# Edits to a recommendation tower: the Gram products by single samples in two runs per block, transposed by VectorE straight from PSUM; unit moves all on ScalarE

## What is computed

```python
e = stack([tbl_f[ids[:, f]] for f in range(26)], axis=1)          # 2048 x 26 x 128
all_emb = concatenate([r_bottom_output[:, None, :], e], axis=1)   # 2048 x 27 x 128
gram = einsum('bfd,bgd->bfg', all_emb, all_emb)
z = gram[:, TRIU_I, TRIU_J]                                       # 351 pairs, k=1
h = concatenate([z, r_bottom_output], axis=1)                     # 479
h = maximum(h @ W_top1 + b_top1, 0)                               # 512
h = maximum(h @ W_top2 + b_top2, 0)                               # 256
y = h @ W_top3                                                    # 1
```

## Time and profile before

| | us |
|---|---|
| three runs | 396.2, 398.02, 399.08 (median 398.02) |
| profiled execution | 398.24, its span 396.4 |
| TensorE clock granted, mean over the span | 0.99 |

### The profile page before, as it was taken

One profiled execution on the slowest core, in us unless ns is written; L12 is line 12 of the kernel. 1 busy time (PEld: TensorE's weight loads), 2 busy tenths in 40 slices (PEclk: granted clock), 3 DMA queues, 4 the chain that ended last, 5 costly groups with the idle time before them and its releaser, 6 DMA issues.

```text
span 396.4 us, 10314 instructions
## 1 busy us (share of the span) xinstructions
PE 364.6 (92%) x4064; PEld 333.9 (84%) x4064; DVE 284.1 (72%) x817; ACT 226.4 (57%) x438; POOL 263.0 (66%) x281
## 2 busy tenths in 40 slices
PE   0878979999998999899979999899998999999997
PEld 0767869988988989799978989799897999998886
DVE  5999998987678776784567676767767687644342
ACT  3446857764654746557654656537465274658841
POOL 6777777777777777657777777777656476576100
PEclk9999999999999999999999999989999899999999
DMA  7656592332232312212332322313112121111000
GB/s 224 196 167 197 162 316 55 82 86 56 55 84 70 89 48 55 68 42 55 84 99 53 89 55 55 101 53 87 48 37 94 33 52 45 41 48 46 19 0 1
DMA packets 16670, 32.17 MB, mean 81 GB/s; under 512 B 5488, under 2 KB 8176, under 8 KB 16496
## 3 DMA queue, kind: packets, MB, share of 16 engines
q0 software_dynamic: 8704, 17.84, 17.5%
q1 hardware_dynamic: 7920, 13.69, 10.8%
HBM read 31.50 MB, written 0.01 MB: 80 GB/s over the span
## 4 chain that ended last, share of the span: by engine, by line
PE 67%; DVE 22%; issue 5%; ACT 4%; DMA 2%; SPq 0%; DVEq 0%
PE hot_ps L367 25%; DVE onehot L518 15%; PE gram_ps L348 14%; PE h_ps L412 8%; PE zh_ps L425 8%; PE xt_ps L333 6%; PE h_ps L409 4%; ACT gram_sb L490 4%; DVE tab L566 3%; DMA stage_sb<-in_hot_dram 2%; DVE XT L478 2%; PE zh_ps L390 2%; DVE h L556 1%; DVE Z L526 1%; PE hot_ps L412 0%
## 5 line engine op out<-in xcount | busy, mean ns | idle before, releaser
L322 POOL DMA_INDIRECT X<-in_table_dram,rows_sb x272 | 261.7, 962 | 104.4 <-issue 77.1
L518 DVE TENSOR_SCALAR onehot<-ids_wide,row_value 128x256 fp32r<-128x256 int16 x640 | 198.4, 380 | 42.1 <-PE hot_ps L367 41.3
L367 PE MATMUL hot_ps<-onehot,tab 128*128 128x256 f32 x1280 | 176.9, 291 | 19.6 <-DVE onehot L518 17.1
L367 PEld LDWEIGHTS hot_ps<-onehot,tab 128*128 128x128 f32 x1280 | 161.7, 194 | 24.6 <-issue 15.4
L490 ACT COPY gram_sb<-gram_ps 32x208 f32<-32x208 f32 x254 | 132.0, 520 | 87.0 <-PE gram_ps L348 70.2
L629 ACT COPY XT<-hot_ps 128x256 f32<-128x256 f32 x72 | 45.3, 635 | 54.1 <-PE hot_ps L367 53.8
L348 PE MATMUL gram_ps<-XT 128*64 128x52 f32 x2048 | 73.1, 223 | 0.2 <-ACT XT L478 0.2
L348 PEld LDWEIGHTS gram_ps<-XT 128*64 128x64 f32 x2048 | 64.9, 138 | 9.3 <-issue 1.2
L412 PE MATMUL h_ps<-stage_sb,w_sb 128*128 128x256 f32 (+3 forms) x198 | 45.1, 363 | 0.0
L425 PE MATMUL zh_ps<-w_sb,stage_sb 128*128 128x256 f32 x128 | 33.6, 409 | 9.2 <-DVE h L556 9.2
L333 PE MATMUL xt_ps<-ident,X 128*128 128x128 f32 x272 | 41.6, 278 | 0.0
(11 more groups left out here) (39 smaller groups left out, 79.3 us busy)
## 6 DMA issues: line engine op xcount, KB each, us to landing
ids_wide<-in_hot_ids_dram SPq DMA_DIRECT2D x14, 320.0 KB, 3.6
X<-in_table_dram,rows_sb POOLq DMA_INDIRECT x272
stage_sb<-in_hot_dram SPq DMA_DIRECT2D x15, 256.0 KB, 3.4
stage_sb<-in_hot_dram SPq DMA_DIRECT2D x10, 192.0 KB, 3.1
bottomT<-in_bottom_t_dram SPq DMA_DIRECT2D x8, 128.0 KB, 3.7
w_sb<-in_w_dram SPq DMA_DIRECT2D x1, 1024.0 KB, 6.0
w_sb<-in_w_dram SPq DMA_DIRECT2D x1, 512.0 KB, 7.9
vec_sb<-in_vecs_dram SPq DMA_DIRECT2D x1, 256.0 KB, 8.2
```

The costliest lines, as they stand in the source:

```text
L322: pool.indirect_dma_start(X[:, n % RING, k, :], None, table, bass.IndirectOffsetOnAxis(idx[:, column:column + 1], 0)).then_inc(gathered[n ...
L367: mm = pe.matmul(hot_ps[i % 2][:, 0:WIDE], tab[u][:, part, D * c:D * (c + 1)], onehot[p % ONEHOTS][:, c - PIECE[u][h], :], start=(c == 0 a ...
L518: compared = dve.tensor_scalar(onehot[p % ONEHOTS][:, c - PIECE[u][h], :], ids_wide[:, u, :], row_value[:, c:c + 1], None, ALU.is_equal)
```

## The change

- `gram` multiplies one sample at a time: 27 columns as weights, 26 moving, into the 27 first partitions of one of four 32-partition quadrants; 32 matmuls per block instead of 16. A tile's Gram lies in two whole banks (16 groups of four samples in each), and waits, at a tile's first block, for the Z transpose of the tile before.
- A block's lookups and Gram are cut in two runs each (`RUNS`): lookups, Gram of 16 samples, lookups, Gram of 16 samples. The last unit of the next block is transposed after the first run of lookups.
- `gram_sb` and `keep_gram` are gone; DVE transposes from `gram_ps` into Z when the tile's Gram is complete.
- All units are moved by ACT, through a single bank `xt_ps`. The bank that this frees holds layer 2's result (`h2_ps`), apart from the transposed Z (`zt_ps`).
- RING 5 to 7, ONEHOTS 3 to 5; XT's slots are no longer padded to 32, and the memset of the padding is replaced by one of `gram_ps`.

```diff
-RING = 5
+RING = 7
-ONEHOTS = 3
+ONEHOTS = 5
-PAIR = 2
-HALF_ROWS = PAIR * PAD
-GROUPS_PER_BLOCK = PAD // 4
+RUNS = 2
+GROUPS_PER_BANK = 16
...
-        XT = sb("XT", [P, XTILES, P, PAD])
+        XT = sb("XT", [P, XTILES, P, SLOTS])
...
-        xt_ps = [ps(f"xt_ps{b}", [P, 512]) for b in range(2)]
+        xt_ps = ps("xt_ps", [P, 512])
...
-        zh_ps = ps("zh_ps", [P, 512])
+        zt_ps = ps("zt_ps", [P, 512])
+        h2_ps = ps("h2_ps", [P, 512])
...
-            def gram(b):
+            def gram(b, run):
 
                 t, j = b // BLOCKS, b % BLOCKS
-                for n in UNITS_OF[b]:
-                    pe.wait_ge(xt_moved[n % 2], n // 2 + 1)
-                if j == 0:
-                    pe.wait_ge(hot_placed, FIRST[t // 2 + 1])
-                    pe.wait_ge(bottom_placed, t + 1)
-                wait(pe, gram_kept, b - 1)
-                for k in range(PAD // PAIR):
-                    pos, rows, at = PAD * j + PAIR * k, HALF_ROWS * (k % 2), PAIR * NG * (k // 2)
-                    pair = XT[:, t % XTILES, pos:pos + PAIR, :]
-                    mm = pe.matmul(gram_ps[rows:rows + HALF_ROWS, b % 2, at:at + PAIR * NG],
-                                   pair.rearrange("d s f -> d (s f)"), pair[:, :, 1:SLOTS], start=True, stop=True)
-                mm.then_inc(gram_full, 1)
+                if run == 0:
+                    pe.wait_ge(xt_moved, UNITS_OF[b][-1] + 1)
+                    if j == 0:
+                        pe.wait_ge(hot_placed, FIRST[t // 2 + 1])
+                        pe.wait_ge(bottom_placed, t + 1)
+                        wait(pe, z_ready, t)
+                count = PAD // RUNS
+                for pos in range(PAD * j + count * run, PAD * j + count * (run + 1)):
+                    group, q = pos // 4, pos % 4
+                    at = NG * (group % GROUPS_PER_BANK)
+                    sample = XT[:, t % XTILES, pos, :]
+                    mm = pe.matmul(gram_ps[PAD * q:PAD * q + SLOTS, group // GROUPS_PER_BANK, at:at + NG],
+                                   sample, sample[:, 1:SLOTS], start=True, stop=True)
+                if run == RUNS - 1:
+                    mm.then_inc(gram_full, 1)
...
             def step(b):
-                for n in UNITS_OF.get(b + 1, []):
+                for n in UNITS_OF.get(b + 1, [])[:-1]:
                     transposes(n)
-                lookup_slice(b)
-                gram(b)
+                lookup_run(b, 0)
+                for n in UNITS_OF.get(b + 1, [])[-1:]:
+                    transposes(n)
+                gram(b, 0)
+                for run in range(1, RUNS):
+                    lookup_run(b, run)
+                    gram(b, run)
                 mlp(b // BLOCKS, b % BLOCKS)
...
             def z_transpose(t):
 
-                dve.wait_ge(gram_kept, BLOCKS * (t + 1) + (1 if t == TILES - 1 else 0))
+                dve.wait_ge(gram_full, BLOCKS * (t + 1))
                 wait(dve, folded_all, t)
-                dve.transpose(Z[:].rearrange("p n m -> p (n m)"), gram_sb[:].rearrange("p n g -> p (n g)")
+                dve.transpose(Z[:].rearrange("p g (b m) -> p g b m", b=2),
+                              gram_ps[:, :, 0:NG * GROUPS_PER_BANK].rearrange("p b (m g) -> p g b m", g=NG)
                               ).then_inc(z_ready, 1)
...
                     z_transpose(t - 1)
                 if j == 2 and t > 0:
                     move_zt(t - 1)
-                moves(b + 1)
                 for p in pieces_ended(b):
                     one_hot(p + ONEHOTS)
...
-            dve.memset(XT[:, :, :, SLOTS:PAD], 0.0).then_inc(pads_zero, 1)
-            dve.memset(zh_ps[:], 0.0).then_inc(pads_zero, 1)
+            dve.memset(gram_ps[:], 0.0).then_inc(pads_zero, 1)
+            dve.memset(zt_ps[:], 0.0).then_inc(pads_zero, 1)
...
             def moves(b):
                 for n in UNITS_OF.get(b, []):
-                    if n % 2 == 0:
-                        move_xt(act, nc.scalar.copy, n)
+                    move_xt(act, nc.scalar.copy, n)
...
-                keep_gram(act, nc.scalar.copy, b, (0, 1) if b == TILES * BLOCKS - 1 else (0, 1, 2, 3))
```

72 lines of the change are left out of this document (23 added, 49 removed).

## The result

The changed kernel takes 382.19 us, the median of four runs (381.81 to 383.99); the kernel before took 398.07 beside it (four runs, 396.2 to 399.08). The ratio is 0.9615, with a 95% interval of 0.9568 to 0.9662: 3.85% faster. The forecast was 384.5. The profiled execution has a span of 380.7 us instead of 396.4, at the same mean granted clock of 0.991.

The account below looks back on a forecast made before the run. The prediction took DVE to bound the start, up to 57 us, and TensorE everything after. From 398.2 us it took 7 (Gram), 3 (start) and 3.5 (one-hot stalls): 384.5 us, range 372 to 404, likeliest case 378 to 391.

Parts of the forecast that it names:

- start: First 57 us, DVE full: three unit moves gone (2.0) and an earlier one-hot piece (1.0), −3 us, bounds −1.5 and −4.
- Gram of 47 blocks: Blocks outside the start, the last 8 and five layer-3 waits: two Gram runs 0.1 us cheaper per block, −4.7 us.
- Gram of the last 8: Blocks of tiles 14 and 15, without lookups, so both runs join: −0.3 us each, −2.4 us.
- one-hot stalls: TensorE's waits for late one-hots after 57 us all go: −3.5 us, bounds −2 and −4.5.
- single xt bank: ACT's unit moves through one bank: 0.59 us each, next transposition a block later, so costed at nothing.
- the Gram's new wait: A tile's first Gram waits for the previous Z transpose: 1.1 us, covered by 2 us or more of other work; nothing.
- r: Time per Gram matmul record on TensorE, two records per fp32 matmul: taken as 10 ns, between 6.3 and 29.7.
- The lower bound, 6.3: Least ns per Gram record if weight columns set the pace: 27 columns, 25 ns per strip, over four strips.
- instruction pace (r 29.7): Rival: instructions, not columns, set TensorE's pace in the Gram; 452 us; chance of the whole slower side 0.2.
- the wash: Rival: r between 12.8 and 15.2, Gram costs 2 to 10 us more, DVE's gains pay; 394 to 402 us, chance 0.15.
- DVE takes over: Rival: one-hot waits not cured by two more buffers, or ACT's later lookup copies replace them; 390 us, chance 0.15.
- The column pace in full, 374: Rival: Gram records at r = 6.5 to 7, with Gram −18 and DVE −6.5: 374 us, chance 0.15.

Follow-up runs that it names:

- experiments 1: The changed kernel with DVE's table splits of blocks 0 to 3 ahead of the same block's one-hots instead of behind: 384.85 us, ratio to the kernel before 0.9666.
- Experiment 2: The changed kernel with three one-hot buffers instead of five: 380.54 us, ratio to the kernel before 0.9559.
- experiment 3: The changed kernel with layer 3 ahead of the one-hots in DVE's list, last block of an odd tile: 372.54 us, ratio to the kernel before 0.9374.
- the second chip: Another chip, where eight follow-up kernels ran and the kernel before takes 504 to 506 us; the changed kernel as it stands was not run there.

## Why the prediction was right, and where it was not

**The sum came out 2.3 us high, and that it was so close is partly luck.** Predicted −3 (start), −4.7 (Gram of 47 blocks), −2.4 (Gram of the last 8), −3.5 (one-hot stalls); measured in the spans +1.1, −8.4, −2.6, −5.0, and two things that had no term: −1.6 for a half-clock stretch and +0.8 for ACT's moves. The forecast had the start 4.1 us better than it came, and the Gram, the stalls and the clock together 6.8 us worse. The direction and the main cause, a cheaper Gram on the engine that bounds the kernel, came as forecast.

**The start: the step that failed.** I took 2.0 for the three moves and 1.0 for the piece ahead of Z. The changed kernel was 2.6 us ahead at block 2, and lost 1.5 us at block 3, 1.2 at block 4 and 1.0 at block 5. The 1.5 come from a cover that the prediction had for the single xt bank, "the move takes 0.59, the next transposition comes a block later". At this block ACT's move stands behind a table split that waits for its load, and TensorE for the move:

```profile
46.88 0.51 ACT L633 CAST tab<-stage_sb 128x384 fp32r<-128x384 f32 x1 [1.46 <-DMA stage_sb<-in_hot_dram]
...
48.10 0.63 PE L329 MATMUL xt_ps<-ident,X 128*128 128x128 f32 x4 [1.87 <-ACT XT L471]
```

The 1.2 come from the cover of the Gram's new wait: "1.1 us after the last Gram against 2 us or more" holds where DVE is free when the Gram ends. At this one tile step it is not, because DVE is full up to there, as the prediction's own first paragraph says. Z's transpose stands behind one-hots and splits, it started at 55.05 us, and the Gram waited 3.24 us. The last 1.0 is the half clock behind that wait (1.05 us over eleven lookups), on which the prediction has no word. The wait for Z is there in experiments 1 (2.1), 2 (1.7) and 3 (2.5) too, so it belongs to the change; the order of the splits is not its cause, and the longer ring adds to it. "The fifth block's Gram some 3 us earlier" was the sign to look for, and it was wrong: 56.24 for the first half, 58.30 for the second, against 57.63. The same kernel's start varies, though: the identical program of experiment 3 was 2.4 us ahead at block 5, 1.1 of it the half clock that it does not have.

**The Gram: right in direction, the term mis-sized by nearly two.** r is 7.5 ns, not 10: nearer to the column reading than I put it. The lower bound, 6.3, had 25 ns per strip from the weight columns; the steady pace is 27.4. That the price goes with the weight columns holds down to 27 (59.4 ns per strip for 64 in the kernel before), and no further: 14 columns take 25.3. A run's way in and out is 0.31 us and not 0.22, since the interval behind the first following matmul is long as well; it is paid once before and twice after, so this costs some 0.1 more a block. Together 1.09 us against 1.22 to 1.27, −0.13 to −0.18; measured by blocks, −0.17 to −0.21. The last 0.03 of that I cannot place. In the blocks around a layer-2 stall, counted at nothing, half of the gain or more was kept (−0.2 to −0.4 for two blocks).

The Trainium skill's floor of some 25 ns between starts ("TensorE: Matmul & The Clock Gate", Wait — 56ns, not 53.3ns?) does not hold for this Gram, whose records start 6.9 ns apart; per strip, at 25.3 and 27.4 ns a round, nothing here goes below it. The same page's figure of about 4 ns between matmuls on different strips (Part 3, Packing small matmuls) is nearer to the 6.3 that the runs show as the least steady pace. The prediction said that the trace of before, at 29.7 ns a record, neither breaks nor proves the floor. That was a mean taken for a spacing: every second record there starts 6 to 8 ns behind the one ahead. These starts already spoke against the rival that TensorE's instructions come every 29.7 ns, to which I gave 0.2.

**The one-hot stalls: 3.5 us forecast, 5.0 measured, from a row read wrongly.** I had taken 7.8 us as waits after 57 us, 17.1 less the first of 9.3. 4.1 of that, though, are eight waits of 0.3 to 0.6 us between 16 and 32 us, where DVE is the bound and nothing could be won, and the changed kernel has its like. After 57.1 us the waits of before list 1.4 us, and 2.1 at 56.99 itself, which is the start's. The rest of the 5.0 are small delays inside groups of lookups that the list does not show. The expected sign, a one-hot wait after the start of under 2 us, is right: none. Experiment 2 shows that the two added buffers have little part in it. What the prediction named beside them, Z's transpose without the wait for ACT and without the move behind it, is what remains to have done nearly all of it.

**Costed at nothing.** ACT's 132 us of copies: rightly nothing. The single xt bank and ACT's later moves: 1.9 us once for the bank (above) and 0.7 us once, TensorE for XT in the step to tile 2, so more than nothing. RING: POOL's wait fell from 25.6 to 1.5 us, and as said nothing that the profile shows followed. No run has the shorter RING; if it matters, then where TensorE waits for gathers, as in experiment 3. Z from PSUM: 1044 ns, nothing, as taken. The memset: 0.91 us instead of 2.19, as said. Layer 2's stall: 9.3 us, as said. The prediction took it as given ("the stall of about 2 us stays"), and it was the largest thing left to take: 9.65 us between the medians for two moved lines, some of it clock and start (experiment 3).

**Of the rivals,** instruction pace (r 29.7) and the wash fell with the first run of 0.233 us. "DVE takes over" described the start and not the rest. The column pace in full, 374, was closer to the truth in r than my own forecast; what kept the time from it is the way in and out. On the second chip the first rival comes true in another form: there TensorE waits for instructions.

## What to carry to other kernels

Small matmuls are cheapest when neighbours lie on different column strips, and what they then cost is as much the entry and exit of each run (0.31 us here) as the matmuls (0.23), so count runs before counting columns. A wait that is covered in steady state needs its cover looked up at every stage, above all where the engine that ends it is full. And before adding buffers, move the short step for which the bound engine waits ahead of the long one on the other engine's list: two moved lines gave more than half of what the whole change had. And look at single starts before a mean is called a pace.
